# Split stationary tiles kept in DRAM for the later strips of a weight fold

## The reference

```python
# first layer: base weights and a low-rank adapter chosen for each batch element
h = einsum('bsi,oi->bso', x, weight) + bias1
h = h + scale[:, None, None] * einsum('bsr,bor->bso', einsum('bsi,bri->bsr', x, a_sel), b_sel)
# second layer: 4-bit codes, one scale for each block of 64
w = (NF4[codes].reshape(-1, 64) * absmax[:, None]).reshape(2048, 2048)
out = x + einsum('bsd,od->bso', h, w) + bias2
```

## Time and profile before

| | |
|---|---|
| median of 3 runs | 2330.23 us (2329.05 to 2330.71) |
| the profiled execution | 2331.05 us |
| its span (first to last instruction) | 2329.3 us |
| TensorE, VectorE, ScalarE busy | 95%, 72%, 48% |
| mean granted TensorE clock | 0.982 |
| moved by DMA | 550.77 MB, 236 GB/s over the span |

### The profile page before, as it was taken

The page is one execution under the profiler, slowest core; times in us unless marked ns, Lnnn a source line. Parts: engine busy times, 40 slices in busy tenths (PEclk is TensorE's granted clock), DMA queues, the critical chain, the costliest instruction groups (busy, mean ns, idle before and its releaser), DMA issues.

```text
span 2329.3 us, 37572 instructions
## 1 busy us (share of the span) xinstructions
PE 2208.8 (95%) x15112; PEld 2013.4 (86%) x15112; DVE 1683.4 (72%) x2400; ACT 1115.0 (48%) x1494; POOL 0.2 (0%) x4
## 2 busy tenths in 40 slices
PE   1179999999999999999999999999999999999999
PEld 1158887887788787899999999999999999999999
DVE  8878987988788544477777776676776666776665
ACT  6656665666566333354444443333434333443432
POOL 0000000000000000000000000000000000000000
PEclk9589999999999999999999999999999999999999
DMA  6128887888688699777777878878888787877775
GB/s 128 61 74 256 269 259 226 252 269 253 211 272 258 207 290 294 236 265 237 229 236 242 257 248 244 245 239 244 283 258 242 244 245 240 291 253 241 241 244 172
DMA packets 399907, 550.77 MB, mean 236 GB/s; under 512 B 41688, under 2 KB 256856, under 8 KB 399608
## 3 DMA queue, kind: packets, MB, share of 16 engines
q1 hardware_dynamic: 399736, 548.38, 75.7%
HBM read 421.93 MB, written 127.42 MB: 236 GB/s over the span
## 4 chain that ended last, share of the span: by engine, by line
PE 55%; DMA 1%; DVE 0%; issue 0%; ACT 0%; SPq 0%; DVEq 0%
PE ps L1033 18%; PE ps L1031 18%; PE ps L1032 18%; PE ps L1074 1%; DMA comb_raw<-wc_d 0%; PE ps L1063 0%; DMA low_d<-low_st 0%; DMA low_st<-low_d 0%; ACT comb L576 0%; DVE res L904 0%; DVE g_b L836 0%; DVE res L882 0%; DVE comb L819 0%; DVE res L897 0%; DVE res L874 0%
## 5 line engine op out<-in xcount | busy, mean ns | idle before, releaser
L1031 PE MATMUL ps<-comb,xs 128*128 128x256 f32 (+1 forms) x3584 | 1015.3, 283 | 1.0 <-issue 1.0
L1033 PE MATMUL ps<-comb,xs 128*128 128x256 f32 (+1 forms) x3584 | 1015.5, 283 | 0.0
L1032 PE MATMUL ps<-comb,xs 128*128 128x256 f32 (+1 forms) x3584 | 1010.0, 282 | 0.0
L581 ACT CAST xs<-xr 128x1024 fp32r<-128x1024 f32 x427 | 447.8, 1050 | 648.1 <-DMA xr<-xc_d 647.8
L825 DVE TENSOR_TENSOR xs<-xr,xs 128x1024 fp32r<-128x1024 f32 x427 | 522.5, 1224 | 311.0 <-ACT xs L581 308.5
L1032 PEld LDWEIGHTS ps<-comb,xs 128*128 128x128 f32 x3584 | 678.5, 189 | 5.2
L1031 PEld LDWEIGHTS ps<-comb,xs 128*128 128x128 f32 x3584 | 677.5, 189 | 1.4 <-issue 1.4
L1033 PEld LDWEIGHTS ps<-comb,xs 128*128 128x128 f32 x3584 | 677.5, 189 | 0.0
L1031 PE MATMUL ps<-wq,tile 128*128 128x512 f32 x1088 | 475.2, 437 | 0.0
L1033 PE MATMUL ps<-wq,tile 128*128 128x512 f32 x1088 | 427.4, 393 | 0.0
L1032 PE MATMUL ps<-wq,tile 128*128 128x512 f32 x1088 | 425.6, 391 | 0.0
(11 more groups left out here) (92 smaller groups left out, 1707.1 us busy)
## 6 DMA issues: line engine op xcount, KB each, us to landing
xr<-xc_d SPq DMA_DIRECT2D x427, 512.0 KB, 4.2
raw<-in_L_cond_weight_dram SPq DMA_DIRECT2D x128, 512.0 KB, 4.5
xc_d<-rq SPq DMA_DIRECT2D x32, 1792.0 KB, 7.6
x_nat<-in_x_dram SPq DMA_DIRECT2D x128, 256.0 KB, 4.0
res<-in_x_dram SPq DMA_DIRECT2D x64, 512.0 KB, 5.6
out_dram<-res SPq DMA_DIRECT2D x128, 256.0 KB, 5.1
wc_d<-cs SPq DMA_DIRECT2D x32, 896.0 KB, 4.6
comb_raw<-wc_d SPq DMA_DIRECT2D x28, 1024.0 KB, 8.3
```

Source lines behind the costliest of these rows:

```text
L581: nc.scalar.copy(xs[f][:, HI, :, :], xr[f][:, LO, :, :]).then_inc(s_xhi, 1)
L1031: nc.tensor.matmul(out_ap, t_hi, m_hi, start=first, stop=False)
L1032: nc.tensor.matmul(out_ap, t_hi, m_lo, start=False, stop=False)
L1033: return nc.tensor.matmul(out_ap, t_lo, m_hi, start=False, stop=last)
```

## The change

In the first strip everything runs as before, and each half tile is stored to a new DRAM tensor `ws_d` once its low half is made: high and low halves together, 2048 floats in each of 128 partitions, contiguous in DRAM. In the three later strips the half is loaded from there, both halves at once, into the same buffers; no cast and no subtraction are issued for them, and TensorE waits for the load. The waits on SP are new as well: a slot whose contents are being stored is not loaded again until the store has landed, and a load waits for the store of its tile.

```diff
+    ws_d = nc.dram_tensor("ws_d", [S1, 2, P, 2 * HK * P], F32).ap()
...
+        s_ws = [sem(f"split_tile_stored{i}") for i in range(4)]
...
                 s = g % S1
+                if 0 <= g - 2 < S1:
+                    sp.wait_ge(s_ws[slot], 16 * ((g - 2) // 2 + 1))
+                if g >= S1:
+                    sp.wait_ge(s_ws[2 * (s % 2) + h], 16 * (s // 2 + 1))
+                    sp.dma_start(tile[slot][:, :, :, :].rearrange("p h k i -> p (h k i)").bitcast(F32), ws_d[s, h]
+                                 ).then_inc(s_ld[slot], 16)
+                    return
...
+            def store_half(g, h):
+                slot = 2 * (g % 2) + h
+                sp.wait_ge(s_lo, 2 * g + h + 1)
+                sp.dma_start(ws_d[g, h], tile[slot][:, :, :, :].rearrange("p h k i -> p (h k i)").bitcast(F32)
+                             ).then_inc(s_ws[slot], 16)
...
             for g in range(JOBS):
                 j, s = divmod(g, S1)
+                if j == 0:
+                    store_half(g, 0)
+                    store_half(g, 1)
...
-                if g + 1 < JOBS:
+                if g + 1 < S1:
                     split_hi(g + 1, 0)
                     split_hi(g + 1, 1)
...
-                if g + 1 < JOBS:
+                if g + 1 < S1:
                     split_lo(g + 1, 0)
                     split_lo(g + 1, 1)
...
-                    if kk == 0:
+                    if kk == 0 and j:
+                        pe.wait_ge(s_ld[slot], 16 * (g // 2 + 1))
+                    elif kk == 0:
                         pe.wait_ge(s_lo, 2 * g + k // HK + 1)
```

## The result

The changed kernel takes 2364.63 us (median of 4, 2360.58 to 2364.93) against 2330.47 for the kernel before: ratio 1.0142, 95% interval 1.0124 to 1.016, some 34 us slower. The forecast was 2370. The profiled execution took 2364.92 us, span 2363.1, 33.8 us more than before.

What follows compares the result with a forecast made beforehand. TensorE's own instructions were taken to bind, with DMA next. First strip 37 us, jobs 15 and 16 12, less 12 absorbed, plus 2 for later strips: +39 us, 2370 us; range 2338 to 2415.

Steps and rivals of the forecast that it cites:

- Part 1: Strips 2 to 4: casts and subtractions removed, 107 us less on ScalarE, 124 on VectorE, worth 0 at the end.
- The byte demand and the rate: First strip, jobs 3 to 14: 5.32 MB a job at 345 GB/s takes 15.4 us against 12.34, 37 us more.
- The lower end, 311 GB/s: DMA engines: lowest rate assumed, 261 GB/s at a share of 0.84 scaled to full; upper end 365 GB/s.
- Jobs 15 and 16: End of first strip: stores plus doubled loads, 6.37 MB a job, 18.5 us each, 12 us more in total.
- Strips 2 to 4: Later strips: doubled loads need 12.4 us a job against 12.34; with uneven demand, 2 us more.
- SP's new waits: SP's queue: waiting for a tile's stores before reloading its slot costs 0.4 us of SP's time, hidden.
- The place of the stalls: First strip: x store starts 5.2 us late behind split stores; TensorE stands about 3 us in each pair.
- queue and bytes are one backlog: First strip: x-store delay and byte total are not added; the byte total gives the larger number.
- Both strips bound: Rival, chance 0.10: at 311 GB/s strips 2 to 4 need 13.7 us a job, +65 beside +61, 2457 us.
- The engines carry it all: Rival, chance 0.11: 8 KB runs move so fast that first-strip jobs fit into 12.34 us, 2330 us.
- Small cost only: Rival, chance 0.12: 365 GB/s or more and a backlog draining in the even jobs, 2340 to 2356 us.
- The clock: Rival, chance 0.07: TensorE's clock falls in the first strip's stalls, +14 us, 2384 us.

Runs made afterwards that it cites:

- relief_only: Changed kernel storing only the first tile; later strips load 0.52 MB halves of it without splitting, so results are incomplete: 2329.83 us, ratio 0.9996.
- spread_even: Changed kernel with the 34 stores spread over two strips, in even jobs only; tiles load split once stored: 2337.01 us, ratio 1.003.
- stores_only: Changed kernel with the first strip's split stores kept, but later strips loading and splitting raw weights as before: 2362.94 us, ratio 1.0139.
- loads_only: Changed kernel storing only the first tile, every split load of the later strips reading that tile: 2330.06 us, ratio 0.9996.
- stores_late: Changed kernel with both split stores of a job queued behind the stores of the weight and x sums: 2371.94 us, ratio 1.018.
- spread_odd: Changed kernel with the 34 stores spread over two strips, in odd jobs, ahead of the x store: 2377.82 us, ratio 1.0199.
- spread_raw2: Stores spread over two strips' even jobs, but the second strip loads raw weights and split loads begin in the third: 2329.85 us, ratio 0.9995.
- kept_warm: Changed kernel with 16 idle matmuls before the third group of transposes in each even job 4 to 16: 2362.13 us, ratio 1.014.

## Why the prediction was right

**Part 1 at 0**: right; relief_only shows it. The busy time that went was 101 and 114 us, where 107 and 124 were forecast.

**The byte demand and the rate.** Demand of 10.6 MB in two jobs was right. I took 345 GB/s; the six pairs ran at 345 to 367, and took 29.6 us on average against the 30.8 forecast. The 12 jobs were to cost 37 us less 6 absorbed, 31; they cost 29.8. That this is so close is in part luck, since two sizes were off and cancel: at the mean rate of 355 GB/s the byte total gives 31.5 us and not 37, and the backlog absorbed little. The six pairs moved 63.2 of the 63.8 MB that they ask for, so 1.8 us of work was put off, not 6. The lower end, 311 GB/s, was not a cap: every pair moved 345 or more. It was an average scaled up from a stretch that was not full. spread_even moved 373 GB/s over 200 us, above my upper end of 365.

**Jobs 15 and 16**: 12 less 6 absorbed were forecast, 7.0 measured; stores_only, which has no doubled loads there, lost 6.7. So the doubled loads of these two jobs cost nothing. They run on into jobs 17 and 18, which move 317 GB/s at a share of 0.84 and keep TensorE busy.

**Strips 2 to 4**: 2 us forecast, 0 measured (loads_only). With them the forecast total of 39 us came to 34.

**SP's new waits**: 0.4 us each were forecast; they were 4.0 us on average, 55.6 us in 14 waits. I had the split stores landed 6.6 us into the job, and one of them alone took 9.3 us to land. That they cost nothing, as forecast, is right for the changed kernel; in stores_late, where they grow to 89.2 us, they reach TensorE.

**The place of the stalls** was forecast (the pair's third group of transposes, some 3 us in a pair, released by the x store) and is what the trace shows: 24.3 us in seven pairs, 3.5 us each. The claim that queue and bytes are one backlog is borne out by spread_odd, whose DMA engines are full (0.97) up to the landing of the x store and slack behind it; that the byte total over two jobs gives the larger number held for the changed kernel alone, since spread_odd asks for no more than spread_even over two jobs and loses 41 us more. In the changed kernel moving the stores in the queue gained nothing, which fits a pace set by bytes. No run keeps spread_odd's bytes in the odd jobs and puts its stores behind the x store; how much of its 2.1 us the order alone would give back stays open.

**The rivals.** Both strips bound (2457): refuted by loads_only. The engines carry it all (2330): refuted, though spread_raw2 shows that it would be right for 8.5 MB a pair. Small cost only (2340 to 2356): refuted; the rate came near its condition, but the backlog did not drain in the even jobs. The 425 GB/s that the Trainium skill gives for a core streaming alone ("HBM Reference", "Specifications (TRN2)") was reached by no run here; the best long stretch read has 384 (kept_warm, 360 to 400 us). The clock (2384): it did fall, to 0.89, 0.89, 0.94 and 0.95 in four pairs, though I had put the stalls down as too short for it and had named a value under 0.95 as a sign that I was wrong. The sign fired and the total still came within 6 us of the forecast. TensorE's matmuls took 10.9 us more; whether that adds to the byte total or hides in it, kept_warm does not settle.

**What I had not seen.** The cost depends on which job of the pair the stores stand in, by 41 us. I worked it out for the x store's lead, but did not draw the conclusion that even jobs, which ask for 2.2 MB less (2.75 MB less in stores, 0.52 MB more of x), were the place for them.

## What to carry to other kernels

Trading engine work for DMA bytes pays only if the engine is on the path; first ask that, then compare the new demand with what the queues have moved at a full share, stretch by stretch and not over the kernel. Where demand is under the cap on average, look at bursts: add up what is queued ahead of a transfer that has little to spare, and ask when it lands with the engines full. Placed in the light job of each pair and spread over two strips, with split loads from the third strip on, the same stores were free. No variant was faster than the kernel before.

## What the runs showed of the hardware

The 16 DMA engines moved 373 GB/s for 200 us (share 1.01, spread_even) and 384 GB/s for 40 us (share 1.00, kept_warm), more than the short windows read of the kernel before (365 at most) and with loads and stores mixed. Stores of 1 MB with 8 KB rows landed in 9.1 to 10.4 us (medians of the runs), where a full queue stood around them. TensorE's granted clock fell for a time to the lower level, 1.2 GHz, in or just behind four of the changed kernel's seven stalls, those of 2.2, 4.4, 5.3 and 5.9 us, and stayed at 2.4 GHz through those of 1.5, 1.6 and 3.4 us: here the length of a stall alone does not say whether the clock falls. With idle matmuls in the place of the stall of 5.9 us the stretch had 1.00 in place of 0.89.
